# Graph attention: four tiles of edges summed in one PSUM bank pair at register offsets, in place of four additions on VectorE

## What is computed

```python
x = _layernorm(x + _L0_gnn_ref(x, src, dst, edge_weight, W1, W2))
x = _layernorm(x + _L1_gnn_ref(x, edge_attr_64, Wq, ..., [src, dst]))

# L0: segment sum of weighted neighbours, then two products
relevant = segment_sum(x[src] * w[:, None], dst)
return relevant @ W1 + relevant * x @ W2

# L1: attention over the edges of each destination
logits = ((q[dst] * k[src]).sum(-1) + (q[dst] * e).sum(-1)) * SCALE
m = segment_max(logits, dst)
ex = exp(logits - m[dst])
attn = ex / segment_sum(ex, dst)[dst]
out = segment_sum(attn[..., None] * v[src], dst) @ Wo + bo
```

## Time and profile before

| | before |
|---|---|
| timed, median of 3 (lowest to highest) | 10865.19 us (10864.79 to 10868.03) |
| span of the profiled execution | 13260.2 us |
| busy TensorE / VectorE / ScalarE / GpSimd | 7727.7 / 5558.1 / 3368.4 / 8204.5 us |
| share of the span | 58 / 42 / 25 / 62 % |
| granted TensorE clock, mean | 0.725 |

### The profile page before, as it was taken

How to read it: one execution, slowest core, us unless ns; L and a number is a source line. 1 busy time by engine, 2 the same in 40 slices (tenths; PEclk the granted TensorE clock), 3 DMA queues, 4 the chain that set the end, 5 groups by cost and what they waited for, 6 DMA issues and landing times. The chain is left out here.

```text
span 13260.2 us, 210680 instructions
## 1 busy us (share of the span) xinstructions
PE 7727.7 (58%) x48566; PEld 6102.5 (46%) x48566; DVE 5558.1 (42%) x20556; ACT 3368.4 (25%) x7806; POOL 8204.5 (62%) x6569
## 2 busy tenths in 40 slices
PE   2444444444444444444577777777777777777777
PEld 1344333334344334333355555555555555555555
DVE  2333333333333333334544444444444454444455
ACT  1111111111111111111233333333333333333333
POOL 3888888888888888886344444444444444444441
PEclk7666666666666666666777777777777777777776
DMA  8666666666666666666555555555555555555552
GB/s 197 106 106 106 106 105 106 106 105 106 106 106 106 106 106 106 106 106 130 182 137 138 139 137 138 136 140 140 138 137 138 138 139 139 140 137 138 137 138 76
DMA packets 2236565, 1660.60 MB, mean 125 GB/s; under 512 B 734074, under 2 KB 1994684, under 8 KB 2236252
## 3 DMA queue, kind: packets, MB, share of 16 engines
q0 software_dynamic: 628992, 668.10, 30.1%
q1 hardware_dynamic: 1538069, 907.12, 24.7%
q10 hardware_dynamic: 69448, 84.72, 1.9%
HBM read 1374.49 MB, written 284.45 MB: 125 GB/s over the span
## 5 line engine op out<-in xcount | busy, mean ns | idle before, releaser
L467 POOL DMA_INDIRECT rel_sum<-sums,row x3224 | 5004.5, 1552 | 1193.1 <-issue 631.8
L1058 POOL DMA_INDIRECT kv<-kv_rows,src_idx x3232 | 3121.7, 966 | 3420.8 <-DVE msg L1280 2494.2
L423 PE MATMUL coef_ps<-same,spread 128*128 128x128 f32 x6448 | 1640.6, 437 | 3528.6 <-DVE spread L396 2914.6
L423 PEld LDWEIGHTS coef_ps<-same,spread 128*128 128x128 f32 x6448 | 1424.2, 325 | 3711.0 <-DVE spread L396 3078.8
L1298 DVE TENSOR_TENSOR acc<-acc,out_ps 128x256 f32 x3232 | 1364.4, 422 | 1946.9 <-remote 911.2
L410 DVE TENSOR_TENSOR row<-moved,src_col 128x8 int32<-128x8 f32 x403 | 69.5, 173 | 3760.8 <-DMA rel_sum<-sums,row 3760.7
L1091 PE MATMUL ring_ps<-pick,q_win 128*128 128x128 f32 x6464 | 1265.6, 351 | 141.6 <-issue 134.3
L1091 PEld LDWEIGHTS ring_ps<-pick,q_win 128*128 128x128 f32 x6464 | 1075.8, 249 | 583.2 <-issue 574.4
L1149 PE MATMUL out_ps<-put,msg 128*128 128x128 f32 x6464 | 1236.2, 350 | 3.8 <-issue 3.8
L396 DVE TENSOR_SCALAR spread<-iota_n,rel_col,w_col 128x128 f32<-128x128 f32 x3224 | 1214.5, 382 | 0.0
L392 DVE SCALAR_TENSOR_TENSOR same<-src_bc,src_col,later 128x128 f32<-128x128 f32 x3224 | 1118.2, 347 | 202.0 <-issue 136.5
(11 more groups left out here) (164 smaller groups left out, 7310.4 us busy)
## 6 DMA issues: line engine op xcount, KB each, us to landing
q_win<-q_rows SPq DMA_DIRECT2D x3232, 64.0 KB
src_bc<-src_flat SPq DMA_DIRECT2D x403, 512.0 KB
x_win<-in_x SPq DMA_DIRECT2D x3224, 64.0 KB
rel<-rel_flat SPq DMA_DIRECT2D x404, 256.0 KB
attr<-in_edge_attr SPq DMA_DIRECT2D x804, 128.0 KB
mark<-marks ACTq DMA_DIRECT2D x202, 256.0 KB
kv<-kv_rows,src_idx POOLq DMA_INDIRECT x3232
rel_sum<-sums,row POOLq DMA_INDIRECT x3224
```

The source lines that it names most:

```text
L423: last = nc.tensor.matmul(coef_ps[k][:, i, :], spread[:, b, j, :], same[:, b, j, :], start=True, stop=True)
L467: pool.indirect_dma_start(out=rel_sum[r], out_offset=bass.IndirectOffsetOnAxis(ap=row[:, b, j:j + 1], axis=0), in_=sums[:, b, j, :], in_of ...
L1058: pool.indirect_dma_start(out=kv[:, 2 * i + u, k * S + s, :], out_offset=None, in_=kv_rows, in_offset=bass.IndirectOffsetOnAxis(ap=src_idx ...
```

## The change

A bank now holds four neighbouring tiles: tile k*4 + s is the s-th tile of bank k. Their windows begin at the tile's first destination, and TensorE adds each tile's product into one bank pair of 512 nodes at the tile's offset from the bank's first node, which it reads from memory into registers. The offsets are made once in `neighbours` and stored in `offs`. The bank is opened by a one-column product of a blank (zero) matrix at column 0, and closed by another at the column behind the last tile's window; only for the very first bank the opening product has 512 columns. The weights of all four tiles write partitions 0 to 7. VectorE adds column 0 to the accumulator and copies the other 511 columns of the weights' bank; ScalarE copies the 511 columns of the messages' bank. `acc` is overwritten and no longer added to, but for that one column. The messages are made in place in `kv`, whose halves come free when the bank is summed (`out_done`). The words and marks are loaded by SyncE, the marks in four DMAs. The order of each engine's steps is another; the order in which the ring banks are filled stays. `prepare` makes and turns a second table of relative destinations.

```diff
-        acc = sb("acc", [P, 2, N])
+        acc = sb("acc", [P, 2, N + NB])
-        out_ps = ctx.enter_context(nc.psum_tensor("out_ps", [P, 2, S, P], F32))
+        out_ps = ctx.enter_context(nc.psum_tensor("out_ps", [P, 2, SP], F32))
 # GpSimd
-                            wait_alone(pool, msg_ready[1], n.plus(-3).count(2, 1 - u), passed)
+                            wait_alone(pool, out_done[2 * u + 1], n.plus(-3).count(), passed)
 # TensorE
                 def out_bank(c, k):
-                    pe.wait_ge(msg_ready[k % 2], c.count(2, 1 - k // 2))
-                    pe.wait_ge(put_ready[k % 2], c.count(2, 1 - k // 2))
-                    wait(pe, summed[k - 1][S - 1], c.plus(-(k == 0)).count())
+                    pe.wait_ge(words_in[c.slot], c.landed(48))
+                    pe.sem_inc(passed, 1)
+                    pe.load(regs, shift[0:1, c.slot, k * S:(k + 1) * S])
+                    past, *later = [pe.snap(r, min_val=0, max_val=top) for r, top in zip(regs, (SP - 1,) + (SP - P,) * 3)]
+                    wait(pe, out_kept[k - 1], c.plus(-(k == 0)).count())
+                    wait(pe, den_kept[k - 1], c.plus(-(k == 0)).count())
+                    for i in range(2):
...
+                            nc.tensor.matmul(out_ps[:, 1 - i, 0:1], blank[:], blank[:, 0:1], start=True, stop=True)
+                        nc.tensor.matmul(out_ps[:, 1 - i, bass.ds(past, 1)], blank[:], blank[:, 0:1],
+                                         start=False, stop=True, skip_group_check=True)
+                    pe.wait_ge(msg_ready[k], c.count())
+                    pe.wait_ge(put_ready[k], c.count())
+                    msg = messages_of(c, k)
+                    columns = [slice(0, P)] + [bass.ds(at, P) for at in later]
                     for s in range(S):
                         lanes = slice(s * Q + k * H, s * Q + (k + 1) * H)
-                        nc.tensor.matmul(out_ps[s * Q:s * Q + H, 1, s, :], weight[:, c.slot, lanes], put[:, k % 2, s, :],
-                                         start=True, stop=True)
+                        nc.tensor.matmul(out_ps[0:H, 1, columns[s]], weight[:, c.slot, lanes],
+                                         put[:, k % 2, s, :], start=False, stop=True, skip_group_check=True)
                     for s in range(S):
-                        mm = nc.tensor.matmul(out_ps[:, 0, s, :], msg[:, k % 2, s, :], put[:, k % 2, s, :],
-                                              start=True, stop=True)
+                        mm = nc.tensor.matmul(out_ps[:, 0, columns[s]], msg[:, s, :], put[:, k % 2, s, :],
+                                              start=False, stop=True, skip_group_check=True)
                     mm.then_inc(out_done[k], 1)
 # VectorE
-                    for s in range(S):
...
-                        win = acc[:, :, bass.ds(start[s], P)]
-                        nc.vector.tensor_tensor(win, win, out_ps[:, :, s, :], ALU.add).then_inc(summed[k][s], 1)
+                    column = acc[:, :, bass.ds(first, 1)]
+                    nc.vector.tensor_tensor(column, column, out_ps[:, :, 0:1], ALU.add).then_inc(joined, 1)
+                    nc.vector.tensor_copy(acc[:, 1, bass.ds(first + 1, SP - 1)], out_ps[:, 1, 1:SP]
+                                          ).then_inc(den_kept[k], 1)
 # ScalarE
+                def keep_out(c, k):
+                    wait_alone(act, words_in[c.slot], c.landed(48), passed)
+                    first, = load_starts(act, first_reg, window[0:1, c.slot, k * S:k * S + 1], N)
+                    act.wait_ge(joined, c.count(B, B - 1 - k))
+                    nc.scalar.activation(acc[:, 0, bass.ds(first + 1, SP - 1)], out_ps[:, 0, 1:SP], ACT.Copy
+                                         ).then_inc(out_kept[k], 1)
```

More of the change, by code:

```diff
@@ L955, in _ @@
                                         ).then_inc(c_b, 1)
-                for i in range(2):
-                    nc.vector.memset(out_ps[:, i], 0.0).then_inc(c_b, 1)
+                nc.vector.memset(blank[:], 0.0).then_inc(c_b, 1)
                 dve.wait_ge(const_ready, 2)
@@ L1074, in attr_fill @@
                     full = n.is_under(NG - 1)
-                    loads = 2 if full else sum(LAST_ROW + (s * B + 2 * u + h) * P < E for s in range(S) for h in range(2))
+                    loads = 2 if full else sum(LAST_ROW + ((2 * u + h) * S + s) * P < E for s in range(S) for h in range(2))
                     if full:
@@ L1344, in body @@
                     if new:
+                        picks(m, 1)
+                    if old:
+                        keep_bank(c, 3)
+                    if mid:
+                        messages(n, 0)
+                    if new:
+                        picks(m, 2)
+                        products(m, 0)
+                    if mid:
+                        carry_decay(n)
+                        messages(n, 1)
+                    if new:
                         products(m, 1)
                         picks(m, 3)
-                    if old:
-                        add_bank(c, 3)
@@ L1349, in body @@
                     if mid:
-                        messages(n, 0)
+                        keep_bank(n, 0)
+                        messages(n, 2)
+                    if new:
+                        products(m, 2)
+                        products(m, 3)
+                    if mid:
+                        keep_bank(n, 1)
+                    if new:
+                        scan_forward(m)
+                        scan_back(m)
                 body(Group(0, -2))
                 body(Group(0, -1))
-                groups(dve, NG, HEAD, TAIL, {1: range(6), 2: (4, 6, 8)}, ((32, 1), (32, 2), (48, 1)), body)
+                groups(dve, NG, HEAD, TAIL, body)
@@ L1436, in body @@
                         weight_copy(n)
+                    if new:
+                        q_drain(m, 1)
+                    if old:
+                        keep_out(c, 3)
+                    if mid:
+                        put_masks(n, 1)
+                    if new:
+                        attr_drain(m, 1)
+                    if mid:
+                        put_masks(n, 2)
+                    if new:
+                        q_drain(m, 2)
+                    if mid:
+                        keep_out(n, 0)
                 body(Group(0, -2))
                 body(Group(0, -1))
[L1440 removed]
+                groups(act, NG, HEAD, TAIL, body)
 def nodes_two(nc, e, acc, den_lane, head_of_t):
```

393 lines of the change are left out of this document (204 added, 189 removed).

## The result

The changed kernel takes 11521.18 us in the median of four runs (11503.05 to 11528.34), the kernel before 10864.99 us in four runs beside them; the ratio is 1.060, with an interval of 1.0585 to 1.0615. That is 656 us more.

A forecast was written before the change was run, and what follows sets the result against it. GpSimd was taken to bound attention before, 20.3 us a group. TensorE's 17.7 plus 2.6 and 1.8 gives 22.1, plus 0.8 and 1.2 gives 24.1, so 11,620 us; own range 11,150 to 12,200, wider range 10,500 to 12,350.

The forecast's parts named there:

- The root: Attention before the change: when timed it runs at GpSimd's pace, 20.3 us a group, with TensorE at 17.7.
- the profiler's load: Attention: the 2395 us by which the profiled execution exceeds the timed runs were taken as stretch from profiling.
- Denominator products: TensorE, each bank: eight records on partitions 0 to 7 run one after another, +0.65 us a bank, +2.6 a group.
- Openers: TensorE, before each bank: sixteen one-column products a group at 0.11 us each, +1.8 us a group (0.8 to 3.4).
- Register loads: TensorE, before each bank: four-word load and address work, mostly hidden, 0.2 us a bank, 0.8 a group (0 to 4.4).
- The wait for the carry: TensorE, after the ends product: waits for VectorE's keep_bank and carry_over with nothing between, +1.2 us a group.
- rival 3: TensorE in attention: register loads fully exposed, 12,460 us, more with stretches at 1.2 GHz; chance 0.11.
- VectorE's saving: VectorE in attention: additions become one column plus a copy, 5.4 us a group less, worth nothing by itself.
- the 5 that the prediction gave as a sign: Attention, sign of being right: VectorE's busy share falls by 5 us a group while TensorE's rises.
- The 0.7 us of cover: SyncE in attention: its work goes from 16.0 to 19.6 us a group, hidden with 0.7 us to spare.
- rival 1: Attention: GpSimd's floor holds after the change, TensorE staying near 20.5 us a group; 10,850 to 10,950 us; chance 0.09.
- rival 2: Attention: the bank's handover between TensorE and VectorE sets the period, so the change is faster, up to some 970 us; chance 0.20.

The follow-up runs named there:

- b_again_2: The kernel before, unchanged, run again for its trace in the faster state of the chip: 10865.7 us.
- b_again: The kernel before, unchanged, run again for its profile in the slower state of the chip: 13273.37 us, ratio 0.9996.
- a_fixed: The changed kernel with fixed bank columns, no register loads or address work, and wrong sums, in the chip's slower state: 13944.51 us, ratio 1.0494 to before.
- a_order: The changed kernel with VectorE's picks earlier and TensorE's q_fill and bank 3 moved around the carry: 11224.14 us, ratio 1.0327 to before.
- b_serial_2: The kernel before with all four denominator products writing partitions 0 to 7, in the chip's faster state: 11082.74 us, ratio 1.0196.
- a_no_openers: The changed kernel without its one-column opening and closing products, some columns computed wrongly: 11224.55 us, ratio 1.0325 to before.

## Why the prediction was right, and where it wasn't

*The root.* The forecast took 20.4 us a group for attention before and measured is 20.5; GpSimd at 20.3 sets it, and TensorE's 17.7 is 17.7 (b_again_2). The reason given for leaving 2395 us of the profile aside, the profiler's load, was wrong (b_again). The number held because the step that located the time was right: the neighbour stage is unstretched, so all of it lies in attention.

*The sum.* Forecast 24.1 us a group, measured 23.8 to 24.0, by terms that were off on both sides:

- Denominator products, +0.65 a bank: measured 0.98 less 0.34, 0.64, which is 2.5 a group. Right. The rule of the strips (the Trainium skill, TensorEngine Tiling (Array Packing), Theoretical Speedup) is borne out by 0.34 against 0.98 us for the same eight records in four strips and in one, 2.9 times where the page has up to 4.
- Openers, +1.8 (0.8 to 3.4): 0.7 in a_fixed, without register work, with starts 0.03 us apart, so the term was below its own range. It was sized by the nearest row, which was too far. The figure of the Trainium skill (TensorEngine Tiling (Array Packing), Instruction Overhead), about 60 cycles, fits these starts, but as a sum, 0.4, it is too low. Taking them out gave 1.45, clock included.
- Register loads, +0.8 (0 to 4.4): about 0.5, the 0.37 between the openers and 0.16 of "issue" before the first one, 23.4 us in 142 groups. The sum was near; the step that failed is "the same load on DVE", 0.95 us, by which all exposed would be 4.4: in before the four words lie apart in the row, in after they lie side by side, and the load takes a third (ns, min/median/max), here TensorE's in after:

```profile
L1217 PEldq TENSOR_LOAD <-at_shift x569: 327/331/351, 7001.8 to 10396.6; - x190
```

- The wait for the carry, +1.2: measured 1.08, and at the drop 0.25 on average.
- The clock, forecast only in rival 3: 1.27 us a group on average, by the blocks behind that wait that run at 1.2 GHz in 81 of 141 groups. a_order, without the wait, has the mean at 0.98.

By these, 17.7 + 2.5 + 0.7 + 0.5 + 1.3 + 1.3 = 24.0. The sum forecast 1.4 us too much for openers and loads and had nothing for the clock, which cost 1.3; that these two cancel is luck. Without the clock's cost the time would have been some 260 us shorter, further from the forecast and still in its range. The lower end of that range, 11,150, doesn't come out of the three low ends that it names: they give 20.7 us a group, 10,930.

*Hidden terms.* VectorE's saving was worth nothing, as said: it now waits 927 us in 3400 for the bank. Its busy time falls from 15.9 to 12.8 us a group, 3.0 and not the 5 that the prediction gave as a sign: its 2.2 us a bank for the additions held their gaps and the handover too. ScalarE's copy takes 0.597 us and is hidden. SyncE was hidden, but mis-sized: 18.1 us a group before, not 16.0, and 22.4 after, not 19.6. The mark issues take 0.83 us each and not the 0.45 of attr:

```profile
9001.44 3.31 SPq L1099 DMA_DIRECT2D mark<-marks  x4
```

and once in three groups SyncE stands for 2.6 us behind its loop branch (first starts 7064.0 and 7066.6, in a_order), where before needs 0.3:

```profile
L838 SPq COMPARE_BRANCH  x50: 54/54/54, 7064.0 to 10360.8; - x50
L838 SPq FUSED_REGOPS  x50: 47/47/47, 7066.6 to 10363.6; - x50
```

The 0.7 us of cover that the prediction gave to SyncE against GpSimd was thus none; what covered it was TensorE at 24.

*The rivals.* GpSimd's floor didn't hold (rival 1): it asked for three terms near their low end, and two were, openers and loads; the denominators and the waits alone, 17.7 + 2.5 + 1.3, make 21.5, above 20.3. The bank's handover (rival 2) isn't the period of before: GpSimd waits there for 50 us in 3400. But it isn't nothing either, as b_serial_2 shows. Register loads exposed (rival 3) fell with 0.33 us a load; the other half of that rival, the clock, came true.

*What was left out.* The sum adds TensorE's terms to its busy time as if its waits of before all vanished. In after no wait of TensorE for VectorE before a bank is left, with VectorE 3.0 us a group lighter; b_serial_2, with VectorE as before, still has 1.6 us of it. That the one is the reason for the other is argued, not shown.

## What to carry to other kernels

Work taken off an engine that isn't the bound gains nothing, and what the new form adds to the next engine is paid in full once that engine becomes the bound. Here VectorE's additions were saved, and TensorE lost its column strips because four tiles write the same eight partitions of the bank. Before taking a price for a small instruction, look at how its operand lies in memory and at what stands before it; and count every queue that a moved DMA joins, with the price of that DMA's own shape. When two savings give no more together than one alone, look for the wait that has grown and for the queue without one: it is probably the next bound. And a price read off one group of a trace can mislead, here for the clock and for the openers.

## What the runs showed of the hardware that was not expected

One chip ran the same kernel at 13,281 and, in a later series, at 10,865 to 10,873 us, and both times steadily (13 runs within 0.15%, 7 within 0.07%). The neighbour stage was the same in both; in attention the releases from TensorE came microseconds late, 822 us of ScalarE's waits in 3400 at transposes already ended, where b_again_2 has ScalarE start 0.04 us after them. What brings this on stays open.

A register load costs by how its words lie. VectorE's and SyncE's in b_again_2, with words apart, and in after, with words side by side:

```profile
L42 DVEq TENSOR_LOAD <-at_window x660: 946/952/982, 7003.7 to 10394.6; - x165
L42 SPq TENSOR_LOAD <-q_start x331: 1700/1900/2072, 7002.1 to 10398.8; - x166
```

```profile
L42 DVEq TENSOR_LOAD <-at_window x711: 299/305/321, 7004.1 to 10399.2; - x178
L42 SPq TENSOR_LOAD <-q_start x285: 520/707/860, 7003.2 to 10399.0; - x143
```

SyncE's is eight words in both, before in four pairs that lie apart, 1.90 against 0.71 us; VectorE's is four words before and one after, and TensorE's four adjacent words in after, 0.33 us, cost hardly more than VectorE's one, 0.31.

And in after TensorE's clock fell to 1.2 GHz, in 81 of 141 groups, behind a wait of 1.1 us that lies between products of a few columns (L1197, L1201, L1206). In a_no_openers the same wait was followed by it in 68 of 151. Before, TensorE waited up to 1.4 us twice a group, behind the full blocks of a q_fill, and in 5 of 164 groups alone a block ran at the lower level. What decides wasn't tried.
